# The up products of every expert tile, made as four column strips of 32 side by side

## The reference

```python
x = layernorm(x + self_attention(x))            # 16 heads of 16, softmax over 1024 keys
x = layernorm(x + cross_attention(x, ctx))      # 77 context rows
x = layernorm(x + experts(x))

# experts: 8 of them, 2 chosen for each token
h = relu(xf @ w1e + b1e)      # 256 -> 1024, the "up" product
y = h @ w2e + b2e             # 1024 -> 256, the "down" product
out += y * weight_of_this_expert_for_the_token
```

## Time and profile before

| what | value |
|---|---|
| median of 3 runs | 1377.91 us (1376.17 to 1378.13) |
| the profiled execution | 1377.51 us, of which the span of instructions is 1375.5 us |
| PE busy | 1350.5 us, 98% of the span |
| PEld busy | 994.9 us, 72% |
| DVE, ACT, POOL busy | 1053.9, 860.3, 612.0 us |
| granted clock | 1.00 until the last 25 us |

### The profile page before, as it was taken

How to read it: one execution, slowest core, us unless ns; L and a number is a source line. 1 busy time by engine, 2 the same in 40 slices (tenths; PEclk the granted TensorE clock), 3 DMA queues, 4 the chain that set the end, 5 groups by cost and what they waited for, 6 DMA issues and landing times.

```text
span 1375.5 us, 49487 instructions
## 1 busy us (share of the span) xinstructions
PE 1350.5 (98%) x18336; PEld 994.9 (72%) x18336; DVE 1053.9 (77%) x2006; ACT 860.3 (63%) x1903; POOL 612.0 (44%) x1061
## 2 busy tenths in 40 slices
PE   9999999999999999999999999999999999999995
PEld 5445445567776776676655547999999999999995
DVE  6888888888888888988999975777665666566663
ACT  4688888888788888788888785663332223333331
POOL 3221121222322323552323532556777776666664
PEclk9999999999999999999999999999999999999998
DMA  6236555444435323433242326333444443333331
GB/s 210 77 102 187 151 168 170 134 110 138 127 99 139 116 65 92 113 94 86 72 155 66 103 70 205 85 96 98 121 129 126 117 118 97 93 96 96 97 93 51
DMA packets 149752, 156.87 MB, mean 114 GB/s; under 512 B 68955, under 2 KB 121498, under 8 KB 148490
## 3 DMA queue, kind: packets, MB, share of 16 engines
q1 hardware_dynamic: 134922, 114.25, 30.7%
q0 software_dynamic: 14016, 38.15, 8.3%
q10 hardware_dynamic: 576, 1.31, 0.3%
HBM read 90.70 MB, written 62.91 MB: 112 GB/s over the span
## 4 chain that ended last, share of the span: by engine, by line
PE 83%; DVE 4%; issue 4%; DMA 4%; POOL 3%; SPq 1%; DVEq 0%; ACT 0%; POOLq 0%; ACTq 0%
PE pa L1103 15%; PE po L1275 14%; PE pa L1349 14%; PE pb L1103 14%; PE pb L1361 13%; PE px L1103 8%; DVE neg L1652 2%; PE pb L1096 1%; PE po L1096 1%; DMA out<-space,y_tags 1%; PE px L1096 1%; DMA o_last<-y_parts,y_tags 1%; DMA space<-reciprocals 1%; POOL y_parts L1044 1%; DMA minus_maxima<-neg_turned 0%
## 5 line engine op out<-in xcount | busy, mean ns | idle before, releaser
L1652 DVE TENSOR_REDUCE neg<-pa 128x1 f32<-128x1024 f32 x512 | 611.6, 1213 | 59.5 <-PE pa L1103 44.9
L1482 ACT ACTIVATE w_sb<-pb 128x512 f32<-128x512 f32 x996 | 590.8, 599 | 100.3 <-PE pb L1103 60.9
L1103 PE MATMUL pb<-w_sb 99*32 99x512 bf16 x3984 | 421.8, 380 | 1.7 <-issue 0.6
L1103 PE MATMUL pa<-w_sb 96*32 96x512 bf16 (+1 forms) x4208 | 338.4, 379 | 4.9 <-DVE neg L1652 4.4
L1580 ACT ACTIVATE space<-pa,b1T_sb 128x128 f32<-128x128 f32 x568 | 154.7, 384 | 298.8 <-PE pa L1349 298.7
L1275 PE MATMUL po<-w_sb,space 128*32 128x256 f32 x4000 | 316.6, 379 | 0.1
L1349 PEld LDWEIGHTS pa<-xgT,attn_t 128*128 128x128 f32 x2272 | 265.2, 192 | 7.5 <-DVE xgT L1958 3.0
L1349 PE MATMUL pa<-xgT,attn_t 128*128 128x128 f32 x2272 | 267.8, 275 | 1.0 <-DVE xgT L1958 1.0
L1361 PE MATMUL pb<-w_sb,space 128*128 x1136 | 260.2, 379 | 0.0
L1361 PEld LDWEIGHTS pb<-w_sb,space 128*128 128x128 f32 x1136 | 209.7, 190 | 25.5
L1103 PEld LDWEIGHTS pa<-w_sb 96*32 96x32 bf16 (+1 forms) x4208 | 132.5, 97 | 103.9 <-DVE neg L1652 31.8
(11 more groups left out here) (272 smaller groups left out, 1244.1 us busy)
## 6 DMA issues: line engine op xcount, KB each, us to landing
y_parts<-attn_t SPq DMA_DIRECT2D x13, 896.0 KB, 4.9
xg<-x_by_expert SPq DMA_DIRECT2D x71, 130.0 KB, 2.2
w_sb<-w SPq DMA_DIRECT2D x17, 512.0 KB, 4.6
attention_out<-space SPq DMA_DIRECT2D x64, 128.0 KB
w_sb<-w SPq DMA_DIRECT2D x7, 1024.0 KB, 7.1
q_parts<-w_sb SPq DMA_DIRECT2D x48, 128.0 KB, 3.2
w_sb<-q_parts SPq DMA_DIRECT2D x64, 96.0 KB, 2.3
w_sb<-k_parts SPq DMA_DIRECT2D x64, 96.0 KB, 2.4
```

The costliest lines, as they stand in the source:

```text
L1103: mm = pe.matmul(out[at:end], lhsT[:, at:end], rhs, start=start, stop=stop, tile_position=(0, at))
L1482: act.activation(ex_of(n)[:, half * HALF:(half + 1) * HALF], score_bank(n, half), ACT.Exp, scale=SCALE).then_inc(e_done, 1)
L1652: dve.tensor_reduce(neg[i % 2][:, t:t + 1], pa[n % 2][:, :], AX.X, ALU.max, negate=True).then_inc(max_done, 1)
```

## The change

The 16 products of each `up` are made by `quarters` instead of by one `pe.matmul` each. `quarters` returns its last product, on which the semaphore is raised as before. Nothing else changes; a disabled branch in POOL's code, which never ran, is dropped too, so that lines behind it have numbers smaller by two (`quarters` L1101, `sums` L1273, `down` L1358).

```diff
                         if f == 0:
                             pe.wait_ge(w1_copied[k], tile + 1)
 
-                        mm = pe.matmul(pH[tile % 2][:, f, :], w1_e[:, k, f * P:(f + 1) * P], xgT[tile % 2][:, k, :],
-                                       start=k == 0 and f % PER_BANK == 0,
-                                       stop=k == KD - 1 and f % PER_BANK == PER_BANK - 1)
+                        mm = quarters(pH[tile % 2][:, f, :], w1_e[:, k, f * P:(f + 1) * P], xgT[tile % 2][:, k, :],
+                                      k == 0 and f % PER_BANK == 0, k == KD - 1 and f % PER_BANK == PER_BANK - 1)
                         if f == FT - 1:
                             mm.then_inc((half_done, up_done)[k], 1)
```

More of the change, by code:

```diff
@@ L994, in _ @@
                         pick_pool(done, s // 5)
-                    if done >= 0 and since == 3 and s == 1 and False:
-                        tags_pool(done)
                     at = TURN * (since - 3) + s - 2
```

## The result

The changed kernel takes 1399.91 us (median of 5 runs, 1399.42 to 1401.09); the kernel before takes 1377.79 us beside it (5 runs, 1376.17 to 1378.13). The ratio is 1.0164, with an interval of 1.0153 to 1.0175: 22 us slower. The profiled span went from 1375.5 to 1397.4 us.

What follows compares the result with a forecast made beforehand. PE's own time was taken to bound the expert part. To the profiled 1377.51 us came 26.7 for changes, less 4 for strips and 0.5 for waits: 1399.7, rounded down to 1399, range 1389 to 1413.

Steps and rivals of the forecast that it cites:

- rival A: Expert part: strips as fast as in the earlier trace, changes at 0.33 us a pair; 1399 us, 1393 to 1406; chance 0.63.
- The price of a pair of changes: On PE, going from whole array to strips and back costs 0.33 to 0.35 us; 0.33 taken.
- Rival E: Late starts at 835 and 25 us were semaphores, so changes cost nothing and strips' gain remains: 1369 to 1374 us; chance 0.06.
- rival D: A change costs less in the tiles than at 835 us, 0.15 us a pair: 1386 us; chance 0.08.
- How it splits: Plain tile of 7.30 us: up to down 3.5 plus 0.21 us, down to up 3.45 plus 0.12.
- The count: PE's program: changes rise from 2 to 83 each way, 81 pairs more, 26.7 us at 0.33 each.
- The gain of strips: Up's 16 products take 3.52 instead of 3.57 us: 0.05 us a tile, 0 to 9 us over 71 tiles, 4 taken.
- Rival C: Up's strips lose pace over long stretches, 0.1 us a tile lost instead of 0.05 gained: 1410 us; chance 0.11.
- The absorbed waits: PE's three waits for DVE can absorb at most 1.0 us of the added time; 0.5 us taken.
- Rival B: Instruction supply binds in up, decided by up over 3.8 us: 1435 us, or 1413 with occasional pauses; chance 0.12.

Runs made afterwards that it cites:

- half of each, once more: Kernel before with four of eight hidden blocks of each up half in strips, rerun where the kernel before takes 1376.98 us: 1419.31 us, ratio 1.0309.
- half of each up: Kernel before with hidden blocks 0 to 3 of every up in strips, 4 to 7 whole, first run on a slower chip: 1491.46 us, ratio 1.0719.
- the one with halves: Kernel before with each up product made as two products of 64 columns side by side, on a slower chip: 1443.82 us, ratio 1.0381.
- the one without reads: Changed kernel without PE's reads of the expert's number, down on one fixed expert's weights: 1398.81 us against 1376.77, ratio 1.016.
- all in strips without reads: Changed kernel with down and token products also in strips, fixed down weights, no PE reads of the expert's number: 1379.06 us, ratio 1.0012 to the kernel before.

## Why the prediction was right

It said 1399 us; 1399.91 was measured, by rival A's mechanism: PE's own time bounds the tail, and each change between strips and whole array costs PE about 0.33 us a pair. Step by step:

**The price of a pair of changes, 0.33 us: right, and shown.** Plain tiles with no pair but all in strips cost -0.07 to -0.08 us, with one pair +0.33 (one product in strips) and +0.26 (all of up), with two +0.67 and +0.63. So the cost goes with the number of changes, not with the work in strips. The Trainium skill, "TensorEngine Tiling (Array Packing)", "Key Properties", says that a change of tiling mode drains the engine; these runs agree: the next form's loads never run ahead, and the pair costs 0.33 us in float32. Rival E (semaphores) is out, since a change with no wait ahead of it costs the same (half of each, once more), and so is rival D (0.15 us).

**How it splits: wrong, without effect on the sum.** I put up's stretch at 3.5 + 0.21 us and down's at 3.45 + 0.12; they are 3.63 and 3.65. Of the 0.21 to 0.23 us that a whole product costs after strips, my own reading of the earlier trace rows had 0.12 ahead of its start and 0.11 behind it, and the part behind belongs to down's stretch: 3.52 + 0.12 = 3.64, and 3.45 + 0.11 + 0.09 = 3.65.

**The count, 81 pairs more: one too many.** One pair shows in a plain tile and two in a token tile; the latter measure 0.31 each, which takes 0.3 us off the 26.7. The pair for `last_reps` in tile 1 was no new one: that tile costs 0.59 more than before (10.29 for 9.70 us), hardly more than the 0.55 of the token tiles without it. The products of `last_reps` have 32 rows, a form of their own, and in the kernel before they already begin 0.09 us behind the last slot of up (848.51), with their loads beside them and not ahead:

```profile
848.60 1.13 PE L1096 MATMUL px<-o_last,cv 32*128 32x256 f32 x4
...
848.60 0.72 PEld L1096 LDWEIGHTS px<-o_last,cv 32*128 32x128 f32 x4
```

So whole products and products of few rows are two forms as well, and a count of changes has to look at both dimensions. That is another 0.3 us.

**The gain of strips, 0.05 us a tile: too small.** It is 0.07 to 0.08 (3.50 us for 16 products), within the bounds of 0 to 0.13; 5.3 us instead of the 4 taken. Rival C is out: 128 records of strips take 3.50 us, with no pace lost.

**The absorbed waits: too small.** I took the idle time in PE's rows, three waits of 1.0 us together, and half of it. But six tiles were longer by 2.2 us than their neighbours (in PEld's rows all six waited for DVE, 3.0 us, in PE's only three), and a slower PE gave back all of that, with 0.4 us more in another tile. "At most 1.0 us" was the wrong reading: to the idle time in a row come the 0.16 us by which the last record outlasts its slot, and 0.10 for a load that isn't ahead.

**Missing: the pauses where two ups stand in a row.** Rival B had the mechanism for each tile and I gave the place with the densest instructions no thought of its own: 512 of them in a row. The first stretch came out 3.1 us longer, where the terms alone would have made it 0.5 shorter (the pair that goes, and the gain of two ups); of these 3.6 us 0.6 stood ahead of `up(0)` already.

**The errors together.** They are of both signs: -2.1 us by the waits, -1.3 by strips, -0.6 by the pairs of the token tiles and of `last_reps`, +3.6 by the first stretch. That takes 0.4 off the predicted 22.2, and 21.9 is measured in the span. So the mechanism was right, but errors of 4 and 3.6 us cancelled each other: that the prediction came out within 1 us is luck. Two slips had no effect. ACT has 4.5 us left when its relu is done (1207.40 to the down at 1211.94 that needs it), not 3.1. And the fetch queue brings 0.75 packets more for each tile (53 for 71), where I put down one.

**Rival B: wrong where the result was taken, right elsewhere.** Its decider was an up in strips of over 3.8 us. On the chips where the kernel before takes 1377 us up is 3.63 in each plain tile. On the one chip with 1391 us on which the changed kernel ran, up took 5.6 us in the tile shown, 3.6 to 9.8 in the plain tiles, and the kernel 1561, far beyond the 1435 that B allowed. The chances were given for one chip, as if chips were alike; on that one the change costs 170 us, not 22.

**What stays open.** What differs between the chips isn't settled, nor whether it is the chip or the time at which it was used; that the supply of instructions is what gives out is read from "issue" as the reason, and not shown by a run of its own. Reads of the expert's number are not what costs on a chip with the good supply; on the others the kernels without reads weren't run. Nor was all in strips tried with the right expert's weights: down's operand is addressed by a register, and in strips it was tried with a fixed address alone. No version here with the right result beat the kernel before.

## What to carry to other kernels

In this kernel products in strips and whole products next to each other on PE cost 0.33 us each time there and back (float32); so put a whole phase into one form, and count the alternations before the gains. With 128 moving columns in float32 strips give 2% of up, 0.07 us, and cannot pay for one alternation in each 7 us. A form with four times as many instructions made the time differ by 11.5% between chips, where it had differed by 1%: look at such a kernel on more than one before it is believed. And read the cost of a wait from the distance between tiles, not from the idle time in its row.

## What the hardware showed that I had not expected

- Chips of one kind, or one kind of chip at different times, differ in how fast strips run: the kernel before, whole in its tail, differs by 1% between them (1391 and 1377 us), most of it (8.8 of 10.6 us in the one pair of traces) ahead of the first down, in the attention part, which is in strips; the one with up in strips differs by 11.5% (1561 and 1400).
- On the slower ones an up in strips often passes at full pace for its first 50 to 80 records, then 1 to 5 come each 0.75 us for two to four rounds, and then the pace returns. ACT's relu began a median of 3.2 us after down's start there in the run with half of each up, and 2.5 in the one with halves; in the kernel before it is 0.3.
- On the others, 192 records with 192 loads in each 6.95 us, 55 instructions in a microsecond, ran through most plain tiles without a pause.
- Even there two ups in strips in a row, 512 instructions, brought a pause of 1.7 to 2.6 us in the rows in each of the four profiles that have this place: the changed kernel's two, the one without reads, and all in strips without reads. In the last two the granted clock was at its lower level for 3.4 us behind the pause, in the first two it stayed up.
- In those four profiles `up(0)` begins at 834.4 to 835.9 us, and the first down at 846.6 to 847.1: where up began earlier, the pauses were longer.
